# A Mamba-2 mixer with a LoRA feed-forward: sums of squares in column tiles, state products one place earlier, high weight parts kept in memory

## What is computed

```python
proj = hidden_states @ in_proj_w.T                       # 8192 gate, 8192 + 2*1024 conv, 128 dt columns
gate, hBC, dt = jnp.split(proj, [INTER, INTER + CONV_DIM], axis=-1)
hBC = silu(conv1d_4_taps(hBC) + conv_b)                  # then hs, Bx, Cx
dt = jax.nn.softplus(dt + dt_bias)
A_cs = jnp.cumsum(A_dt, axis=-1)                         # per chunk of 128 tokens
M = Gm * Lmat                                            # (C B^T) * exp(segsum), per head
Y_diag = jnp.einsum('bclsh,bcshp->bclhp', M, X)
states = jnp.einsum('bclhn,bclhp->bchpn', B_decay, X)
new_states = jnp.einsum('bzjh,bzhpn->bjhpn', decay_chunk, states)
Y_off = jnp.einsum('bclhn,bchpn->bclhp', Cc, prev_states) * sdo[..., None]
y = (Y_diag + Y_off).reshape(b, L, H, P) + D_res
xg = y.reshape(b, L, INTER) * jax.nn.silu(gate)
xr = xg.reshape(b, L, G, INTER // G)                     # G = 8 groups of 1024 channels
xr = xr * jax.lax.rsqrt(jnp.mean(xr * xr, axis=-1, keepdims=True) + EPS)
out = (xr.reshape(b, L, INTER) * norm_weight) @ out_proj_w.T
```

## Time and profile before

| | |
|---|---|
| median of 3 runs | 1606.25 us |
| the profiled execution | 1604.1 us, its span 1602.4 us |
| PE busy, matmuls in the profile | 1578.8 us (99%), 9172 |
| DVE, ACT, POOL busy | 1423.1, 1370.4, 1279.1 us |
| granted PE clock | full in all 40 slices but for the last few us |
| DMA | 311.83 MB, 63.9% of the 16 engines' span on SP's queue |

### The profile page before, as it was taken

One profiled execution on the slowest core, in us unless ns is written; L12 is line 12 of the kernel. 1 busy time (PEld: TensorE's weight loads), 2 busy tenths in 40 slices (PEclk: granted clock), 3 DMA queues, 4 the chain that ended last, 5 costly groups with the idle time before them and its releaser, 6 DMA issues. The chain is left out here.

```text
span 1602.4 us, 29224 instructions
## 1 busy us (share of the span) xinstructions
PE 1578.8 (99%) x9172; PEld 1296.0 (81%) x9172; DVE 1423.1 (89%) x2328; ACT 1370.4 (86%) x2620; POOL 1279.1 (80%) x1614
## 2 busy tenths in 40 slices
PE   9999999999999999999999999999999999999998
PEld 7877888888888888887778788888888888888886
DVE  7989899999999998999979888888888898888887
ACT  4688899999999898988846899989999999899895
POOL 5549998989898998989874487877777777778786
PEclk9999999999999999999999999999999999999999
DMA  5266767677767676676614666766766677667662
GB/s 175 93 186 205 227 188 218 201 209 214 195 218 206 201 224 199 206 206 198 196 40 145 204 208 200 225 202 202 227 189 218 207 204 222 199 205 227 190 218 89
DMA packets 231754, 311.83 MB, mean 195 GB/s; under 512 B 144176, under 2 KB 160560, under 8 KB 231344
## 3 DMA queue, kind: packets, MB, share of 16 engines
q1 hardware_dynamic: 231600, 309.97, 63.9%
HBM read 240.69 MB, written 36.70 MB: 173 GB/s over the span
## 5 line engine op out<-in xcount | busy, mean ns | idle before, releaser
L409 ACT ACTIVATE mt<-cs_row,cs_tok 128x128 f32<-128x128 f32 x1024 | 324.9, 391 | 0.0
L633 POOL TENSOR_TENSOR wl<-raw,wh 128x256 fp32r<-128x256 f32 x328 | 254.4, 807 | 59.3 <-ACT wh L381 59.3
L727 POOL COPY xt<-turned 128x512 uint16<-128x512 uint16 x248 | 206.3, 878 | 58.6 <-DMA turned<-tg 58.2
L718 POOL TENSOR_TENSOR mt<-mt,gt 128x256 f32<-128x256 f32 x128 | 117.8, 942 | 134.3 <-ACT mt L590 134.3
L743 POOL TENSOR_TENSOR sqa<-sqa,sq 128x256 f32<-128x256 f32 x222 | 221.6, 1018 | 0.8 <-ACT sq L563 0.8
L750 POOL TENSOR_TENSOR wol<-raw_o,woh 128x256 fp32r<-128x256 f32 x256 | 183.3, 737 | 39.0 <-ACT woh L530 38.9
L736 POOL TENSOR_TENSOR xl<-xg,xh 128x256 fp32r<-128x256 f32 x254 | 192.2, 778 | 5.1 <-ACT xh L543 5.1
L1093 DVE SCALAR_TENSOR_TENSOR cv<-bt,par_sb,cv 128x511 f32<-128x511 f32 (+2 forms) x192 | 143.8, 749 | 42.5 <-ACT cv L385 37.9
L1093 DVE SCALAR_TENSOR_TENSOR cv<-bh,par_sb,cv 128x511 f32<-128x511 f32 (+2 forms) x192 | 143.7, 748 | 30.8 <-ACT cv L385 25.8
L1323 DVE TENSOR_TENSOR mt<-mt,gt 128x1024 f32<-128x1024 f32 (+1 forms) x128 | 159.7, 1247 | 0.9 <-ACT mt L590 0.9
L381 ACT ACTIVATE wh<-raw 128x1024 fp32r<-128x1024 f32 (+1 forms) x146 | 151.9, 1040 | 0.8 <-DMA raw<-in_w_dtag 0.8
(11 more groups left out here) (217 smaller groups left out, 3819.2 us busy)
## 6 DMA issues: line engine op xcount, KB each, us to landing
raw<-in_w_step SPq DMA_DIRECT2D x128, 512.0 KB, 4.5
cs_row<-cs_rows SPq DMA_DIRECT2D x128, 512.0 KB, 7.0
low_parts<-wl SPq DMA_DIRECT2D x64, 512.0 KB, 5.8
raw_o<-in_w_out SPq DMA_DIRECT2D x128, 256.0 KB, 5.7
wl<-low_parts SPq DMA_DIRECT2D x64, 512.0 KB, 4.7
ec_row<-ec_rows SPq DMA_DIRECT2D x256, 96.0 KB, 5.7
raw<-in_w_bc SPq DMA_DIRECT2D x16, 512.0 KB, 3.5
acc<-in_x SPq DMA_DIRECT2D x8, 256.0 KB, 5.0
```

What stands on the lines that cost most here:

```text
L409: e = act.activation(mt[:, m % 2, h, chunk(j)], cs_row[:, m % 2, h, chunk(j)], ACT.Relu, bias=cs_tok[:, j, 2 * m + h:2 * m + h + 1], scale ...
L633: e = pool.tensor_tensor(wl[:, n % 2, cols], raw[:, n % 2, cols], wh[:, n % 2, cols].bitcast(F32), ALU.subtract)
L727: e = pool.tensor_copy(to[:, half], turned[:, NJ * half:NJ * (half + 1), :])
```

## The change

Three things are changed together.

- Sums of squares: instead of `sqa` as the stationary operand and one column of ones moving, a 128x32 block of ones is stationary and `sqa` moves through it, in four products that write to four groups of 32 partitions of the bank (four column tiles). The sums then lie along the columns, in rows that repeat 32 times. DVE's `mean_square` therefore works on 128x128 elements (`ms_rows`), and a DVE transpose of 32x32 blocks (`ms_cols`) brings the sums back to one per partition. Both lie in `part`, so `mean_square` also waits for the last adding of `part`.
- State products: from step 2 on, PE issues the three state products (L1023) before the third part of `output` (`xl*woh`) and not behind it. They then wait for `xd` alone; the wait for `xt` (`v_x`) moves to L1033.
- High parts: a new tensor `high_parts` in memory. In the first batch SP stores each `wh` (`keep_high`) as the last transfer of each step, and ACT waits before it overwrites a `wh` block until its store has landed. In the second batch SP loads `wh` in place of `raw` (`load_parts`), PE waits for that load, and ACT's 64 splits for the steps are gone.

With them POOL's `add_drained` in the second batch moves: all three blocks in the first step of a group, ahead of `wol`.

```diff
 def load_parts(m):
     if m < 2:
         sp.wait_ge(t_c, did(GROUPS + (GROUPS - 2 + m)))
     else:
         sp.wait_ge(t_g, did(STEPS + m - 2))
+    sp.wait_ge(st_high[m % 2], landed(m))
+    sp.dma_start(wh[:, step(1, m) % 2, :].bitcast(F32), high_parts[m]).then_inc(ld_high[m % 2], 16)
     sp.wait_ge(st_low[m % 2], landed(m))
     sp.dma_start(wl[:, step(1, m) % 2, :].bitcast(F32), low_parts[m]).then_inc(ld_low[m % 2], 16)
...
+def keep_high(m):
+    sp.wait_ge(a_wh, did(step(0, m)))
+    sp.dma_start(high_parts[m], wh[:, step(0, m) % 2, :].bitcast(F32)).then_inc(st_high[m % 2], 16)
...
-                    if m + 2 < STEPS or b + 1 < NB:
+                    if b + 1 < NB:
                         load(step(b, m + 2))
...
+                    if b == 0 and has(m + 1):
+                        keep_high(m + 1)
...
             def split_hi(n):
+                b, m = step_of(n - 2)
+                if b == 0 and m >= 0:
+                    act.wait_ge(st_high[m % 2], landed(m))
                 act.wait_ge(ld_raw[n % 2], landed(n))
...
+                    if b + 1 == NB and has(m - 2) and m > 2 and (m - 2) % PER_GROUP == 0:
+                        add_drained(b, (n - 2) // PER_GROUP - 1, range(ACT_BLOCKS))
                     if has(m - 1):
                         pool.wait_ge(a_woh, did(n - 1))
...
+                    early_state = has(m) and has(m - 2) and by_dma(b, m - 1)
+                    def sum_squares(dst, src, start=True, stop=True):
+                        of = src[:, :].rearrange("p (j a c) -> p a j c", j=NJ, c=SQ)
                         for a in range(P // SQ):
+                            mm = pe.matmul(dst[SQ * a:SQ * (a + 1), 0:P].rearrange("p (j c) -> p j c", j=NJ), ones[:, :],
+                                           of[:, a], start=start, stop=stop)
+                        return mm
...
                         if has(m - 2):
-                            output()
+                            output(range(2) if early_state else range(3))
...
                         pe.wait_ge(v_xd, did(n - 1))
-                        pe.wait_ge(v_x, did(n - 1))
+                        if not by_dma(b, m - 1):
+                            pe.wait_ge(v_x, did(n - 1))
...
                         mm.then_inc(t_st, 1)
+                        if early_state:
+                            output((2,))
                         yb = bank_y(b, m - 1)
+                        pe.wait_ge(v_x, did(n - 1))
...
             def mean_square(g, src):
                 dve.wait_ge(t_ss, did(g))
-                dve.tensor_scalar(ms[:, :], src[:, 0:NJ], 1.0 / (INTER // GROUPS), 4 * EPS, ALU.mult, ALU.add).then_inc(v_ms, 1)
+                dve.wait_ge(p_acc, did(g - 1, ACT_BLOCKS))
+                dve.wait_ge(p_lo, g // GROUPS + 1)
+                dve.tensor_scalar(ms_rows, src[:, 0:P], 1.0 / (INTER // GROUPS), 4 * EPS, ALU.mult, ALU.add).then_inc(v_some, 1)
+                dve.wait_ge(v_some, did(g))
+                dve.transpose(ms_cols, ms_rows).then_inc(v_ms, 1)
```

More of the change, by code:

```diff
@@ L58 @@
 SQ = 32
-TURN_FROM = 0
 def mixer_kernel(nc, x, w_step, w_bc, w_dtag, w_out, par, headpar, w_ffn, w_b, b_ffn, b_gate, out):
@@ L592, in _ @@
                             take_b(b, GROUPS - 1)
-                    if has(m) and not early_split and (has(m + 2) or b + 1 < NB):
+                    if has(m) and not early_split and b + 1 < NB:
                         act.wait_ge(t_g, did(n))
@@ L976, in output @@
                         else:
-                            for k, (a, c) in enumerate(parts):
+                            for k in ks:
+                                a, c = parts[k]
                                 wait_low(k)
@@ L1065, in _ @@
                         pe.wait_ge(a_sq, did(n - 2))
-                        for j in range(NJ):
-                            pe.matmul(bt[:, j:j + 1], sqa[:, chunk(j)], ones[:, 0:1], start=True, stop=False)
-                            mm = pe.matmul(bt[:, j:j + 1], sq[:, chunk(j)], ones[:, 0:1], start=False, stop=True)
-                        mm.then_inc(t_ss, 1)
+                        sum_squares(bt, sqa, stop=False)
+                        sum_squares(bt, sq, start=False).then_inc(t_ss, 1)
                         output()
```

94 lines of the change are left out of this document (34 added, 60 removed).

## The result

| kernel | median of the runs | range | main loop from, us | span of the profiled execution |
|---|---|---|---|---|
| before | 1605.24 us | 1604.5 to 1606.3 | 102.76 | 1602.4 |
| after | 1581.05 us | 1580.7 to 1581.6 | 103.86 | 1579.3 |

The change makes the kernel faster: ratio 0.9849, 95% interval 0.9834 to 0.9863, 24.2 us. The forecast was 1590 with a range of 1582 to 1602, so the direction was right and the gain a third too small. In the profiled executions it is 1604.1 against 1581.05, 23.05 us, where the sum had 16.6. "Main loop from" is the start of step 2, the first step in which all three stages run.

A forecast was written before the change was run, and what follows sets the result against it. PE was taken as the bound, busy 1578.8 of 1602.4 us, so only its work and waits count. Terms of -16.6 took the profiled 1604.1 to 1587.5; 2.15 from profiled execution to median made it 1590, range 1582 to 1602.

The forecast's parts named there:

- the -1.7: At the first batch's two ends: PE's waits for POOL's `xl` go, saving 1.7 us.
- The three steps around the drain: End, first and second step of first-batch groups: gain 0.28 + 0.23 = 0.5 us together, not the 1.6 held.
- DVE comes to `yo` 0.28 earlier than now: End step: with its S 0.2 earlier, DVE reaches `yo` 0.28 us earlier, while PE would allow 0.5.
- The queue: First batch, SP's queue: storing high parts delays steps whose turn already starts behind unfinished loads, costing 3 us in all.
- Rival A: First batch, each step: the transpose waits behind the new store, 0.5 us a step, 31 us, 1618; chance 0.10.
- POOL's order: Second batch, second step of a group: adding fills POOL's idle time before `woh`, so late `xl` goes, gaining 0.56 us.
- The 0.15 for late states in the first step: Second batch, first step of a group: DVE being 0.5 later makes the states later, costing 0.15 us.
- the extra change of type: PE, each step: one more change between fp32r and fp32, taken as 0.03 us, 0.24 per group.
- B: PE, each step: the extra change of type costs the full 0.10, 8.7 us more, 1599; chance 0.10.
- C: Sums of squares: column tiles don't overlap, some 5 us less gain, 1595; chance 0.08.
- E: State products, both batches: moving them brings nothing because the states bind at once, 1600; chance 0.06.
- D: First batch: the store hides wholly and DVE catches up within a group's first step, 3 + 3 us more, 1584; chance 0.10.

The follow-up runs named there:

- forward_only: The kernel before with only the state products moved ahead of the `xl` group, waiting for `xd` alone; median 1588.9 us, 16.5 us faster.
- no_transpose: The kernel after without the DVE transpose in the mean square, so its scales are not the right ones; 1581.1 us.
- longer_dve: The kernel after with two more 128x128 DVE transposes in each end step's mean square, ahead of `yo`; 1583.9 us.
- no_high: The kernel after without the high parts and without POOL's other order; 1581.0 us.
- after_again: The kernel after, unchanged, run again as the measure for the kernels beside it on another chip; 1582.03 us.
- after_third: The kernel after, unchanged, run once more as the measure for two later kernels on their chip; 1581.74 us.
- two_stores: The kernel after with each high part's store issued twice, the second into a tensor nobody reads; 1587.9 us.
- order_only: The kernel before with only POOL's adding moved ahead of `wol` in the second batch, ACT still splitting weights there; 1603.3 us, 3.1 us faster.
- one_tile: The kernel after with four more products behind the sums of squares at 15 places, all into the same column tile; 1592.2 us.

## Why the prediction was wrong

The median is 1581.05 us where 1590 was forecast, 8.95 less. Of this 6.45 us are in the sum (23.05 instead of 16.6), 2.15 in what I added for the distance of the profiled execution to its median, the rest is rounding. By the forecast's own places, profiled execution against profiled execution; the step starts are those of L804 and L820:

| place | forecast | measured |
|---|---|---|
| up to the first end step | part of the -1.7 | +1.1 (180.71 to 181.84) |
| six groups of the first batch | -6.3, queue +3.0 | -10.05 (534.78 to 524.73) |
| from there to the second batch's loop | -0.3, rest of the -1.7 | -1.2 |
| second batch's loop | -10.6 | -11.7 (662.56 to 650.82) |
| tail | -0.7 | -1.2 |
| together | -16.6 | -23.05 |

**Where it failed: the six groups of the first batch**, which gave 6.75 us more than forecast (3.75 in the groups, 3.0 in the queue), where 6.45 are missing in all; the other places cancel. Two terms of them were mis-sized.

*The three steps around the drain*, "thus gain 0.28 + 0.23 = 0.5 together and not the 1.6 that their waits and the sum hold". They gained (11.83 - 11.13) + (11.32 - 11.08) + (11.21 - 10.97) = 1.18 by the medians, 0.7 a group more than said, over 4 us. The failed step is "From `yo` on DVE works without a pause to `xt`, and PE waits for it": the three steps were taken as one rigid row of DVE, in which PE's wait could shrink by 0.23 once. forward_only shows it by itself. There `yo` still waits for PE, and the three steps gain 0.16 + 0.34 + 0.43 = 0.93, not 0.23. The row gave way at two points: its pieces aren't fixed (`mt` 1.22 us there instead of 1.64), and in the second step DVE had a pause of 0.5 us before `cv`, so, as I read it, the wait of that step could go too. What the sums add to that is 1.18 - 0.93 = 0.25, close to the 0.28 said, but not for the reason said.

"DVE comes to `yo` 0.28 earlier than now" failed as well. It came 0.67 earlier, counted from the start of the end step (459.43 - 447.31 = 12.12 before, 454.71 - 443.26 = 11.45 after): its states began 0.30 earlier instead of 0.2, and from the first of the two new operations to `yo` are 0.55, 0.39 and not 0.49 more than the 128x4 one took. So DVE is there with L1069, as no_transpose and longer_dve show, and not 0.22 behind. The sums save 0.54 in the end step (11.67 in forward_only to 11.13); of it 0.10 comes back in the first step, where `mt` took 1.51 us against 1.22 in forward_only, and 0.19 in the second, where PE waits 0.2 at L1069.

*The queue*, +3.0. The store takes 1.6 us of it, where I had 1.35 to 1.5; but with one store the median turn lands as early as before. Between no_high and the kernel after lie 0.1 us a group in this profile, 0.7 in all, and up to 2.8 in the profiles of after_again and after_third (87.57 and 87.79 over six groups, against 87.33 of no_high). The rows of one late turn were a true picture of a seldom case: I took one turn in five, the trace has 2 of 42. With the store it is 7 of 43, so the 3.0 us were not from nowhere; the price was too high for this execution and near that of after_third, whose `xd` waits for a turn three times. Rival A's mechanism was right and its price far off: two_stores is its case, at 3.2 us of stores per step, and costs 6.9 us, not 31. Its median turn lands 1.1 us later, not 3.2; that only what doesn't fit the step delays the turn agrees with both kernels, but wasn't tried by itself.

**Right sum, wrong owner: the second batch.** -11.7 against -10.6, near in part by luck. I gave 0.56 of each group's 1.45 to POOL's order. order_only shows the 0.43 that it can give; but the moved `xl` group hides the same wait (forward_only: 10.77), and no_high has the same 86.82 us as the kernel after. I had said that the forward order "hides all ordinary waits for POOL's `xl`", and then counted the one behind the drain apart. The 0.15 for late states in the first step didn't come (10.99 and 11.00).

**Right:** the sums' eight entries take 0.35 (forecast 0.4), the extra change of type 0.03, the load of `wh` is hidden, the ordinary waits are gone, and rivals B, C and E didn't come. C: the sentence on the mechanism in the Trainium skill, page "TensorE: Matmul & The Clock Gate", section "The mechanism", would have kept the sums near 0.9, since column tiles share their row group; one_tile measured 0.24 against 0.97 for four tiles against one. D came closest and was given 0.10: its 1584 is 3 us off, of which the 2.15 us for the distance of a profiled execution to its median explain most. The kernel after has no such distance: its profile is at the median, and that of before was an early start. D's mechanism was half right: the store hides nearly wholly, but DVE doesn't catch up within the first step (11.08 and 10.97 us in the first and second step, where 10.78 is bare).

Whether `mt` and `xd` are slower because POOL works beside them was not tried. The trace of the kernel before goes with it: between 180 and 640 us `mt` took 1.22 to 1.23 us in all 26 cases in which POOL worked for less than half of it, and 1.61 to 1.77 in the 11 in which POOL worked nearly throughout; but in forward_only some of 1.21 us stand beside a busy POOL too. The Trainium skill, page "GPSIMD Engine Reference", section "1. Specifications", lists POOL's path to SBUF as shared with DVE's instructions of two SBUF inputs, which `mt` and `xd` are. The 26 and 11 cases agree with it; no run here isolates it.

## What to carry to other kernels

Ask of each wait whether the operation behind it reads that data: here a wait moved from one matmul to the next, with nothing reordered, gave 13 us alone, where the whole change gave 24. When several edits each remove a wait, price them together, one after the other, since the second finds the wait already gone; and leave one out to see if it still earns its place (the high parts don't). A chain of an engine can't be shifted as a block: read at the point where two engines meet (here `yo`) which comes last, and by how much, and ask of each piece behind it if its length is the same everywhere and if the engine pauses there.

## What the runs showed of the hardware

- Four 128x32 products into four column tiles of one bank take 0.24 us, from the first one's start to the next group's; into one tile they take 0.97.
- A DMA transpose behind a full queue starts as soon as behind an empty one (1.2 us after its issue), but lands after 4.2 us instead of 3.1.
- In the first batch of the kernel after the same DVE product of 128x1024 took 1.21 to 1.86 us, and the one of 128x384 0.65 to 1.14, at different places of one program.
- A DVE transpose of 128x128 f32 takes 0.31 us, 0.24 to the next operation's start.
- The start of the same program, up to the main loop, varied by 0.9 us over three executions of the kernel after (103.86, 104.00 and 104.77).
